# The second chunk's down products cut up by tiles, the D term as a transpose of a scaled input, and the last norm by pairs of blocks, in a fused scan-and-MLP block

## The reference, cut to what is computed

```python
x = L0_attn_x                                   # (1, 2048, 256)
mod = (silu(c) @ wmod)                          # sa, ca, ga, sb, cb, gb: six vectors of 256
h = layernorm(x) * (1 + ca) + sa
# selective scan, state size 16, over the 2048 tokens:
#   dt, B, C = split(h @ x_proj_w.T); delta = softplus(dt @ dt_proj_w.T + b)
#   s[n] = exp(delta * A[n]) * s[n] + delta * B[n] * h     for n in 0..15
#   y = sum over n of C[n] * s[n]  +  D * h               <- the D term
x = x + ga * y
h = layernorm(x) * (1 + cb) + sb
g = (h @ gate_w.T) * gate_s;  u = (h @ up_w.T) * up_s     # 704 wide
x = x + gb * ((silu(g) * u) @ down_w.T) * down_s          # the down product
```

## Time and profile before

| | |
|---|---|
| median of 3 runs | 303.89 us (302.24 to 305.20) |
| the profiled execution's own time | 301.67 us |
| its span, first to last instruction | 299.8 us |
| mean granted TensorE clock | 0.892 of full |
| busy, share of the span | DVE 87%, PE 82%, POOL 76%, ACT 64% |

### The profile page before, as it was taken

The page is one execution under the profiler, slowest core; times in us unless marked ns, Lnnn a source line. Parts: engine busy times, 40 slices in busy tenths (PEclk is TensorE's granted clock), DMA queues, the critical chain, the costliest instruction groups (busy, mean ns, idle before and its releaser), DMA issues. The chain is left out here.

```text
span 299.8 us, 3877 instructions
## 1 busy us (share of the span) xinstructions
PE 244.5 (82%) x1242; PEld 184.9 (62%) x1242; DVE 261.4 (87%) x337; ACT 193.2 (64%) x314; POOL 227.1 (76%) x114
## 2 busy tenths in 40 slices
PE   7874799968356996877499999972899988987993
PEld 7632598556235564655396677651877767765762
DVE  4589977699999999999999999989999999974651
ACT  2697642975585696797645976884366597526650
POOL 1006799959999999999998999799869999930000
PEclk9995558989758799898979999998699997999999
DMA  7919998149436374468141673581896740002002
GB/s 248 351 35 175 155 150 215 19 77 222 132 90 154 57 157 99 90 103 138 38 125 50 143 153 102 114 145 31 173 182 200 141 97 0 2 0 70 0 2 74
DMA packets 34437, 33.81 MB, mean 113 GB/s; under 512 B 14960, under 2 KB 21488, under 8 KB 34416
## 3 DMA queue, kind: packets, MB, share of 16 engines
q1 hardware_dynamic: 34000, 32.73, 49.4%
q10 hardware_dynamic: 416, 0.81, 0.8%
HBM read 31.12 MB, written 2.36 MB: 112 GB/s over the span
## 5 line engine op out<-in xcount | busy, mean ns | idle before, releaser
L732 POOL TENSOR_TENSOR drv<-u,brow 128x1024 f32<-128x1024 f32 x63 | 147.7, 2361 | 19.0 <-DMA brow<-bc_dram 18.9
L971 ACT ACTIVATE decay<-delta,A 128x512 f32<-128x512 f32 x128 | 87.5, 687 | 68.1 <-DVE state L1151 66.3
L1151 DVE TENSOR_TENSOR_SCAN state<-decay,last,drv 128x512 f32<-128x512 f32 x96 | 118.7, 1267 | 3.8 <-ACT decay L971 3.5
L1528 PE MATMUL sums<-ident,drv 128*128 128x128 f32 x512 | 75.2, 301 | 2.0 <-POOL drv L744 1.3
L1528 PEld LDWEIGHTS sums<-ident,drv 128*128 128x128 f32 x512 | 66.0, 157 | 12.5 <-issue 7.3
L744 POOL TENSOR_TENSOR drv<-state,crow 128x1024 f32<-128x1024 f32 x29 | 68.4, 2363 | 6.0 <-DVE state L1151 6.0
L1125 DVE TENSOR_TENSOR drv<-state,rows_ps 128x1024 f32<-128x1024 f32 x35 | 41.9, 1196 | 3.8 <-PE rows_ps L1502 3.7
L1502 PE MATMUL rows_ps<-c_parts,sel 64*128 64x512 f32 x35 | 19.2, 547 | 28.5 <-DVE drv L1125 28.5
L1151 DVE TENSOR_TENSOR_SCAN state<-decay,drv 128x512 f32<-128x512 f32 x32 | 37.8, 1209 | 3.4 <-ACT decay L971 2.1
L1423 PE MATMUL side<-h_hi,ffn_hi 128*128 128x512 f32 x74 | 26.2, 436 | 5.7 <-DVE h_lo L1075 2.2
L1502 PEld LDWEIGHTS rows_ps<-c_parts,sel 64*128 64x128 f32 x35 | 7.1, 202 | 36.7 <-DVE drv L1125 25.2
(11 more groups left out here) (176 smaller groups left out, 330.4 us busy)
## 6 DMA issues: line engine op xcount, KB each, us to landing
brow<-bc_dram SPq DMA_DIRECT2D x31, 512.0 KB, 5.5
crow<-bc_dram SPq DMA_DIRECT2D x13, 512.0 KB, 6.7
resid<-in_x SPq DMA_DIRECT2D x4, 512.0 KB, 5.3
out<-resid SPq DMA_DIRECT2D x8, 256.0 KB, 3.3
gates<-in_wmod ACTq DMA_DIRECT2D x1, 768.0 KB, 5.8
gates<-in_wmod SPq DMA_DIRECT2D x1, 768.0 KB, 8.4
last<-state SPq DMA_DIRECT2D x48, 1.0 KB, 2.8
crow<-bc_dram SPq DMA_DIRECT2D x3, 256.0 KB, 3.5
```

The costliest lines, as they stand in the source:

```text
L732: nc.gpsimd.tensor_tensor(drv[j % RING_DRV][:, :, 0:S], u[:, c % 2, :, 0:S], b.unsqueeze(1).to_broadcast([P, HALVES, S]), ALU.mult).then_i ...
L971: nc.scalar.activation(decay[i % RING_DECAY][:, 0:S], delta[:, c % 2, h, 0:S], ACT.Exp, scale=A[:, h * N + n:h * N + n + 1]).then_inc(deca ...
L1151: nc.vector.tensor_tensor_scan(state[j % RING_STATE][:, h, 0:S], decay[i % RING_DECAY][:, 0:S], drv[j % RING_DRV][:, h, 0:S], before, ALU. ...
L1528: ins = nc.tensor.matmul(sums[:, b * D + h * P:b * D + (h + 1) * P], of[:, h, b * P:(b + 1) * P], ident[:, :], is_transpose=True, start=Fa ...
```

## The change

Three parts.

1. **Downs of chunk 1.** Instead of four blocks at slots 18 and 21 there are two pairs of blocks, each cut in three: `a` is tiles 5 and 0, `b` is tile 1, `c` is tiles 2, 3, 4. The first stands in slots 14, 15 and 17, the second in 19, 20 and 20. The two `out` of DVE move one slot ahead.
2. **D term.** `diag_D` is gone. ACT multiplies `hmod` in place by the column `Dg` (`Dx0`, `Dx1`, 128x512 each, 8 in all), once `u`, `z` and `bc` have read it, and TensorE transposes the result into `sums`.
3. **Closing of chunk 3.** The last product on DVE, the additions, `x2` (now `half0`, `half1`), the statistics and `rstd` go by halves; `nmr` and `xn` go from POOL and ACT to DVE; `hi1` goes to DVE; gate 0 and up 0 run their high parts before their low parts; `rounds` (ACT) moves behind the last decay; the table load moves ahead; eight idle transposes stand before the gates.

```diff
 LATER = {
     "vector": [
-        (19, "K out0"), (22, "K out1"),
+        (18, "K out0"), (21, "K out1"),
     "tensor": [
-        (18, "K down0"), (18, "K down1"), (21, "K down2"), (21, "K down3"),
+        (14, "K down0a"), (15, "K down0b"), (17, "K down0c"), (19, "K down2a"), (20, "K down2b"), (20, "K down2c"),
...
-                elif name[:4] == "down" and c == NCH - 2:
-                    pair = int(name[4:]) // 2
+                elif name[:4] == "down" and c > 0:
+                    pair = int(name[4]) // 2
                     pe.wait_ge(down_scaled, 2 + FULL + 1)
-                    to, full = take(("K down", c, pair))
-                    for j in (FULL, *range(FULL)):
+                    if name[5:] in ("", "a"):
+                        to, full = take(("K down", c, pair))
+                    else:
+                        to, i, k = side_bank(("K down", c, pair))
+                        full = side_full[i]
+                    for j in {"": (FULL, *range(FULL)), "a": (FULL, 0), "b": (1,), "c": (2, 3, 4)}[name[5:]]:
...
+                elif name in ("Dx0", "Dx1"):
+                    h = int(name[2:])
+                    act.wait_ge(Dg_ready, 1)
+                    act.wait_ge(*u_made(c))
+                    act.wait_ge(*filled(("F z", c, HALVES - 1)))
+                    act.wait_ge(*filled(("F bc", c, 0)))
+                    nc.scalar.activation(hmod[:, c % 2, h, 0:S], hmod[:, c % 2, h, 0:S], ACT.Copy, scale=Dg[:, h:h + 1])\
+                      .then_inc(hmod_scaled, 1)
...
             def add_dterm(c):
-                pe.wait_ge(diag_ready, 1)
-                for h in range(HALVES):
-                    pe.wait_ge(*emptied(("F xT", c, h)))
+                pe.wait_ge(hmod_scaled, HALVES * (c + 1))
...
-                                               hmod[:, c % 2, h, b * P:(b + 1) * P], diag_D[:, h, :],
+                                               hmod[:, c % 2, h, b * P:(b + 1) * P], ident[:, :], is_transpose=True,
...
+                elif name in ("half0", "half1"):
+                    q = int(name[4:])
+                    dve.wait_ge(*((added, upto_added(c, N - 1)) if q else (half_added, 1)))
+                    to = resid[:, BLK0[c] + 2 * q:BLK0[c] + 2 * q + 2, :]
+                    nc.vector.tensor_tensor(to, to, sums[:, 2 * q * D:(2 * q + 2) * D].rearrange("p (b d) -> p b d", d=D),
+                                            ALU.add).then_inc(x2_ready, 1)
...
+                elif name == "h2T" and c == NCH - 1:
+                    to = [take((f"{kind} {name}", c, h)) for h in range(HALVES)]
+                    for q in range(NPAIR[c]):
+                        pe.wait_ge(xn_ready[kind], PAIR0[c] + q + 1)
```

More of the change, by code:

```diff
@@ L217 @@
 KEEP_WARM = 5
+KEEP_WARM_LAST = 8
 RING_DRV = 12
@@ L309, in bank_uses @@
                 elif name[:4] == "down":
-                    blk = int(name[-1])
-                    uses = [(("K down", c, blk // 2), place["K down"][blk // 2])] if blk % 2 == 0 else []
+                    blk = int(name[4])
+                    uses = [(("K down", c, blk // 2), place["K down"][blk // 2])] if blk % 2 == 0 and name[5:] in ("", "a") else []
                 elif name in ("warm", "wb1", "wb2"):
@@ L317, in bank_uses @@
                     uses = [(("F z", c, int(name[1])), PLACE_FIRST["F z"][int(name[1])])]
+                elif name[-1] in "HL":
+                    uses = [((key[:-1], c, 0), place[key[:-1]])] if name[-1] == "H" else []
                 else:
@@ L848, in side_work @@
                       .then_inc(rstd_ready[kind], 1)
+                elif name in ("rstd0", "rstd1"):
+                    q = int(name[4:])
+                    b = slice(2 * q, 2 * q + 2)
+                    act.wait_ge(meanvar_ready[kind], c + 1 + q)
+                    nc.scalar.activation(logvar[kind][:, b], meanvar[kind][:, b, 1], ACT.Ln, bias=eps[:, :])\
+                      .then_inc(logvar_ready[kind], 1)
+                    act.wait_ge(logvar_ready[kind], c + 1 + q)
+                    nc.scalar.activation(rstd[kind][:, b], logvar[kind][:, b], ACT.Exp, scale=-0.5)\
+                      .then_inc(rstd_ready[kind], 1)
                 elif name[:2] == "xn":
@@ L1023, in side_work @@
                     q = int(name[2:])
+                    if kind == "K" and c == NCH - 1:
+                        dve.wait_ge(x2_ready, c + 1 + q)
                     for b in range(2 * q, 2 * q + 2):
@@ L1413, in side_work @@
                     pe.wait_ge(h2_hi_ready, HALVES * (c + 1))
-                    to, full = take((f"K {name}", c, 0))
-                    for part in (h2_hi, h2_lo):
+                    if h2_hi in parts:
+                        to, full = take((f"K {name}", c, 0))
+                    else:
+                        to, i, k = side_bank((f"K {name}", c, 0))
+                        full = side_full[i]
+                    for part in parts:
                         for k in range(HALVES):
@@ L1523, in add_state @@
                     add_dterm(c)
+                of = drv[j % RING_DRV]
+                if (c, n) == (NCH - 1, N - 1):
+                    for h in range(HALVES):
+                        pe.wait_ge(*(upto_prod(c, n) if h else (half_made, 1)))
+                        for b in range(NBLK[c]):
+                            ins = nc.tensor.matmul(sums[:, b * D + h * P:b * D + (h + 1) * P],
+                                                   of[:, h, b * P:(b + 1) * P], ident[:, :], is_transpose=True,
+                                                   start=False, stop=b % 2 == 1 and h == HALVES - 1)
+                            if (b, h) == (1, HALVES - 1):
+                                ins.then_inc(half_added, 1)
+                    ins.then_inc(added, 1)
+                    return
                 pe.wait_ge(*upto_prod(c, n))
-                of = drv[j % RING_DRV]
                 for b in range(NBLK[c]):
```

78 lines of the change are left out of this document (62 added, 16 removed), and 11 rows, old and new, of tables (FINAL, FIRST, PLAN).

## The result

| | before | after |
|---|---|---|
| median | 303.11 us (4 runs, 302.24 to 305.20) | 308.95 us (4 runs, 307.21 to 312.56) |
| ratio after to before | | 1.0165, 95% interval 1.0102 to 1.0228 |
| profiled execution: own time, span | 301.67, 299.8 | 312.56, 310.6 |
| mean granted clock | 0.892 | 0.858 |

The changed kernel is slower by 1.0 to 2.3%, inside the forecast range and on the forecast side.

What follows compares the result with a forecast made beforehand. VectorE's instruction stream was taken as the bound, with GpSimd's chain setting the time from 221 us to the last scan. 301.67 + 6.0 + 0.65 + 1.0 - 2.0 = 307.3, plus 0.57: 307.9 us, range 302.9 to 311.8.

Steps and rivals of the forecast that it cites:

- A: Main case: the bank wait holds the row 4.3 to 7.5 us late, total 305.0 to 310.0, chance 0.58.
- The bank wait holds the row: Near 209 us: first down piece waits for bank 1, holding the row for n = 15; VectorE stalls 6.0 us.
- 3.4 at half: After TensorE's idle near 209 us: clock stays at 0.50 for 3.4 us, doing 1.7 of the queued work.
- my 5.35: TensorE's work from the first down piece through the row for n = 15: 5.35 us at full clock.
- Out 0 ahead of the statistics: Behind the stall, out 0 before the statistics' second half delays rstd, nmr and GpSimd's chain: plus 0.65 us.
- The term of hi 0: ACT's hi 0 holds one decay, about 0.3 us of VectorE; counted as nothing because GpSimd sets the time.
- The D term: Chunk 0: shorter D term gives minus 2.0 at best, plus 2.4 if the clock stays half; taken plus 1.0.
- Rival B: Not slower: clock full by 47.5 in chunk 0, D term gains 1.0 to 2.0; 304.9 or 303.2 us, chance 0.26.
- The closing: Chunk 3's end: no rounds wait, work by halves, high parts first: minus 2.0 us, ends 1.3 and 2.6.
- The base: Starting time: profiled execution of before, 301.67 us, plus 0.57 because the other runs stood above it.

Runs made afterwards that it cites:

- E1: Kernel before with only the downs of chunk 1 cut in pieces and moved, out 0 and out 1 one slot ahead: 313.15 us, ratio 1.0362.
- E2: Kernel before with only the D term changed, to a transpose of the input scaled by ScalarE: median 302.10 us in two groups, ratio 0.9930.
- E3: Kernel before with only the closing of chunk 3 changed: 300.26 us, ratio 0.9913.
- E5: Changed kernel with the old downs of chunk 1, keeping the new D term and closing: median 302.88 us, ratio 0.9897.
- E4: Changed kernel with the first two pieces of the first down pair two slots and one slot later: 303.21 us, ratio 0.9965.
- E7: Changed kernel with the first down pair of chunk 1 in bank 2 in place of bank 1: 306.84 us, ratio 1.0169.
- E8: E4 with out 0, out 1 and the store of out 1 back in the slots of before: 311.26 us, ratio 1.0250.
- E6: E5 with the eight transposes of the D term of chunk 0 run twice: 300.69 us, ratio 0.9923.
- E9: E5 with chunk 0's last twelve one-column products behind the first half of F z, VectorE's copy two scans later: 298.86 us, ratio 0.9854.
- E10: E3 with the same move of the one-column products as E9: 298.89 us, ratio 0.9839.

## Why the prediction was right

The forecast case was A, and A is what happened. By the medians the parts seem to add up: before 303.4, E1 +9.8, E2 -1.3, E3 -3.1 make 308.8, measured 308.95. That it fits to 0.2 is luck, as E2's median falls in its lower group by one execution: by the means it is 303.3 + 10.0 + 0.3 - 3.0 = 310.6, measured 309.4, and E5, parts 2 and 3 together, is 0.7 below before where E2 and E3 promise 4.4. Step by step:

- **The bank wait holds the row** (predicted 6.0, ends 4.3 and 9.7): right in cause and place, too small by 1.5. 7.51 in after, 7.26 in E1. What failed is "3.4 at half": I took the rise of the clock from before, where TensorE did other work at another time. The half clock lasted over 6 us in after. With the windows above, 6.2 us at 0.50 and 2.4 at 0.86 make 5.2 us of work at full clock, so my 5.35 for the work itself was right. I also read before's own 3.4 too short, by the 0.7 from 210.76 to 211.45, which is the smaller part of the miss: 0.35 of stall. (The product that wants the row stands two instructions behind hdn 3, not three; the times in the prediction are right.) E4 and E7 show the mechanism from both sides: the row ahead of the pieces removes it, another bank shortens it by what that bank is free earlier. The rows show no matmul that passes the waiting ones. By the Trainium skill's rule in the prediction (TensorE: Matmul & The Clock Gate, "What happens when you issue a matmul") it had to be so, and the trace agrees.
- **Out 0 ahead of the statistics** (0.65): 0.57 in after (5.47 less 4.90), 0.60 between E4 and E8.
- **The term of hi 0, 0.3 for one decay with GpSimd as the cover, counted as nothing**: failed in size. The wait is 1.03 in after (a scan at 242.04), and GpSimd waits 0.60 for VectorE at 273.19, with 0.36 in E1. From `nmr` to the end of GpSimd's last product it is 45.09 in after and 44.86 in E1, before 44.45. GpSimd had no slack to give. E8 shows what this chain costs if it is let grow.
- **The D term** (plus 1.0, ends -2.0 and +2.4): the executions fall to either side of it, and not evenly as far as the ends. E2's upper group is 1.8 to 5.7 above before's median; undisturbed, lowest against lowest, the D term gives between 0.5 (E2) and 1.3 (E5 against E3), not the 2.0 of the good end. In the profile of after it is the bad one: 3.41 less 1.26 of setup is 2.15 lost. Rival B's condition, L1290 at full speed, came true in the profile of E7 (1.40 at 46.53), which is even so slower than before's (303.38 to 301.67); for the changed kernel itself no trace shows it. TensorE was busy 100% of 44 to 53 us in after at 0.50. The Trainium skill (same page, "The HAM clock gate") says that sustained activity releases the throttle; for those 9 us, in which the profile counts TensorE as busy throughout, the trace doesn't agree.
- **The closing** (-2.0): -1.8 in after, -1.96 in E3's profile, -3.1 in its median. Right in size and by the steps that I gave for it.
- **The base**: I added 0.57 for the profiled execution's luck. The larger sets put before at 303.4 to 304.3, so 1.7 to 2.6 would have been right. It was offset by E2's and E3's medians, which are better than my terms.

That the sum came within 1.1 us rests on offsets: part 1 was short by 3.2 (6.65 against 9.8, the stall and the closing of E1) and the base by 1.2 (302.2 against 303.4), the D term too dear by 2.3 and the closing by 1.1. The 2.1 behind the last scan in E1, a fall of the clock in the closing, stood nowhere in the prediction. A slip without weight: VectorE is at 9 tenths from the ninth slice on, not from the seventh, and the two slices read over, 7 and 6, are chunk 0, where the D term stands.

## What to carry to other kernels

Before work is moved into an engine's idle time, ask what the moved instruction waits for, and read what is queued behind it on that engine: TensorE's idle 7 us were free, but not for an instruction that waited for a bank with a wanted row behind it. Where an engine's time is set by a clock that may or may not have risen, a shorter task is not sure to end sooner; look at single executions, since a median hides two groups. What gained here was work taken out from ahead of a waited-for result.

## What the runs showed of the hardware

I had not expected the granted clock of chunk 0 to be a matter of luck with sides so far apart. In the profiles it rises between about 46 and 49 us in before, E1, E3, E4, E6, E7, E9 and E10, and only from 54 on in after, E2, E5 and E8 (in the last it is still 0.50 in the window from 53 to 56), never between. The late ones all have the D term once and the twelve one-column products ahead of the row; E4 and E7 have these too and were early, so these two don't decide it alone. One program seems to do either: the times of E2, E4 and E5 fall in two groups, though each has a trace of one group only. In the late ones TensorE was busy 100% of the time from 44 to 54 us by the profile, and that did not bring the clock back; in all four it came back while the products of `F z` ran (128x512, from 51.6 to 52.9 on). What decides between the two sides stays open; what is shown is that with the D term kept long (E6) or the one-column products moved away (E9) none of 12 and none of 6 executions was in the upper group.

Setup has a like choice: eight transposes at 11 us took 1.07 in most profiles and 1.95 in after, E4 and E6. ScalarE's first decay began at 24.5 to 24.8 there and at 23.5 in before, but it began as late in E5, E8, E9 and E10 (24.7 to 25.3), where the transposes took 1.07. So they are not all of it, and what decides it stays open.
